# Two-layer cross-attention kernel, cross phase: the place of the attention products and of the last head's transposes in TensorE's order

## The reference, cut to what matters

```python
z = _mha(x1, context, Wq2, Wk2, Wv2, mask1, causal=False)
x2 = _layernorm(x1 + z, ln2_g, ln2_b)
z = jnp.maximum(x2 @ fc1_w.T + fc1_b, 0.0) * mask0
z = (z @ fc2_w.T + fc2_b) * mask0
return _layernorm(x2 + z, ln3_g, ln3_b)
# in _mha, for 16 heads of 32 channels:
energy = einsum('bhsk,bhtk->bhst', Q, K)
lengths = sum(energy[:, :, 0, :] != 0, axis=-1)
energy = where(cols >= lengths, -inf, energy)
out = einsum('bhst,bhtk->bhsk', softmax(energy / sqrt(32)), V)
```

## Time and profile before

| | |
|---|---|
| three runs | 2805.86, 2807.34, 2809.14 us, median 2807.34 |
| profiled execution | span 2805.9 us from first to last instruction, its own time |
| busy share of the span | PE 97%, PEld 84%, DVE 67%, ACT 58%, POOL 23% |
| TensorE's granted clock | 0.996 on average |
| cross phase | about 1963 to 2806 us, a turn of the loop some 51.03 us |

### The profile page before, as it was taken

One profiled execution on the slowest core, in us unless ns is written; L12 is line 12 of the kernel. 1 busy time (PEld: TensorE's weight loads), 2 busy tenths in 40 slices (PEclk: granted clock), 3 DMA queues, 4 the chain that ended last, 5 costly groups with the idle time before them and its releaser, 6 DMA issues.

```text
span 2805.9 us, 68735 instructions
## 1 busy us (share of the span) xinstructions
PE 2723.5 (97%) x24272; PEld 2360.1 (84%) x24272; DVE 1882.0 (67%) x5544; ACT 1634.7 (58%) x4949; POOL 637.8 (23%) x755
## 2 busy tenths in 40 slices
PE   6999999999999999999999999999999999999997
PEld 5888888887888888888888888888888888888886
DVE  6778778777544443445377777777677767767766
ACT  6878877888211111111277777777666666656664
POOL 1111111111000000000023333333233424324333
PEclk9999999999999999999999999999999999999999
DMA  3333332333302112012021111113111111101100
GB/s 119 108 99 99 106 112 86 106 107 99 124 30 60 45 45 60 30 60 88 33 83 51 47 45 45 45 45 105 36 45 37 37 45 45 39 36 45 45 30 24
DMA packets 145494, 178.45 MB, mean 64 GB/s; under 512 B 16272, under 2 KB 75664, under 8 KB 144912
## 3 DMA queue, kind: packets, MB, share of 16 engines
q1 hardware_dynamic: 145424, 177.53, 19.7%
HBM read 121.92 MB, written 55.57 MB: 63 GB/s over the span
## 4 chain that ended last, share of the span: by engine, by line
PE 40%; DVE 5%; issue 2%; ACT 2%; POOL 1%; POOLq 0%; DVEq 0%; ACTq 0%
PE cross_work L172 15%; PE causal_work L172 7%; PE cross_probsT L1961 2%; PE cross_attended L1980 2%; PE cross_scores L1940 2%; PE cross_scores L1961 2%; PE causal_attended L1980 1%; PE causal_scores L1961 1%; PE causal_scores L1940 1%; PE causal_probsT L1961 1%; PE cross_scores L1889 1%; DVE causal_scores L1323 1%; POOL causal_y L610 1%; PE causal_probsT L1922 1%; PE cross_probsT L1922 1%
## 5 line engine op out<-in xcount | busy, mean ns | idle before, releaser
L2804 ACT ACTIVATE mlp_h<-mlp_f,mlp_b1col 128x512 f32<-128x512 f32 x128 | 88.3, 690 | 526.7 <-PE mlp_f L3002 526.7
L3002 PE MATMUL mlp_f<-mlp_xT_hi,mlp_w 128*128 128x512 f32 x1024 | 335.1, 389 | 0.0
L3020 PE MATMUL mlp_acc<-mlp_w,mlp_hT_hi 128*128 128x512 f32 x1024 | 315.2, 389 | 0.0
L2905 DVE CAST mlp_hT_hi<-mlp_h 128x512 fp32r<-128x512 f32 x128 | 57.7, 451 | 375.3 <-ACT mlp_h L2804 375.2
L790 ACT ACTIVATE mask_prob<-mask_scores,mask_low 128x256 f32<-128x256 f32 x512 | 237.1, 475 | 21.5 <-DVE mask_low L1323 21.2
L790 ACT ACTIVATE cross_prob<-cross_scores,cross_low 128x256 f32<-128x256 f32 x512 | 237.5, 499 | 7.2 <-DVE cross_low L1317 7.0
L1323 DVE CUSTOM_DVE_ANT_0 mask_scores<-mask_scores,mask_mask 128x256 f32<-128x256 f32 x512 | 201.4, 457 | 46.4 <-PE mask_scores L1940 46.4
L172 PE MATMUL causal_work<-causal_xT_hi,causal_w 128*128 128x256 f32 x1008 | 227.6, 297 | 0.5
L3020 PEld LDWEIGHTS mlp_acc<-mlp_w,mlp_hT_hi 128*128 128x128 f32 x1024 | 192.3, 188 | 40.0
L3002 PEld LDWEIGHTS mlp_f<-mlp_xT_hi,mlp_w 128*128 128x128 f32 x1024 | 192.3, 188 | 39.8
L790 ACT ACTIVATE causal_prob<-causal_scores,causal_low 128x128 f32<-128x128 f32 (+1 forms) x512 | 211.3, 436 | 19.6 <-DVE causal_low L1323 19.6
(11 more groups left out here) (339 smaller groups left out, 8254.1 us busy)
## 6 DMA issues: line engine op xcount, KB each, us to landing
cross_x_in<-after_attention SPq DMA_DIRECT2D x17, 512.0 KB, 3.7
mask_x_in<-in_x SPq DMA_DIRECT2D x16, 512.0 KB, 4.7
mask_c_in<-in_ctx SPq DMA_DIRECT2D x16, 512.0 KB, 5.6
mask_res<-in_x SPq DMA_DIRECT2D x16, 512.0 KB, 3.6
after_attention<-mask_res SPq DMA_DIRECT2D x16, 512.0 KB, 2.8
mlp_x<-after_attention SPq DMA_DIRECT2D x8, 1024.0 KB, 5.6
mlp_stage<-in_L_xattn_fc_w SPq DMA_DIRECT2D x8, 1024.0 KB, 5.6
after_layer<-mlp_y SPq DMA_DIRECT2D x8, 1024.0 KB, 4.3
```

Source lines behind the costliest of these rows:

```text
L2804: act.activation(h32[:, m % 2, :], F1[m % 2][:], ACT.Gelu, bias=b1col[:, m:m + 1]).then_inc(s["gelu"], 1)
L3002: ins = pe.matmul(F1[m % 2][:], W[2 * (m // 4)][:, a, k, m % 4 * P:(m % 4 + 1) * P], xT[p][:, k, :], start=(k == 0 and n == 0), stop=(k == ...
L3020: ins = pe.matmul(ACC[t][:], hT[a][:, m % 2, t * P:(t + 1) * P], W[2 * (m // 4) + 1][:, p, m % 4, :], start=(m == 0 and n == 0), stop=(m = ...
```

## The change

The same instructions run on every engine, with another order on TensorE and two swaps on ACT; no instruction, wait value, tile or DMA is added or taken away. On TensorE, in the cross phase:

- T(-1) moves ahead of S(0), and A(-1) directly behind S(0); queries and keys follow as one run of 24 matmuls.
- The second half of `values(b, 0)` moves behind T(2); T(3) moves ahead of S(1); A(0) directly behind S(1), and queries behind A(0).
- T(10) moves up to directly behind A(1). The two halves of `feed1(b, 1)` stand behind it with OT(1) between them. T(11) stands behind the second half and ahead of S(3); A(2) directly behind S(3).
- T(14) moves ahead of the keys at the turn's end.
- A(1) is not moved to S(2).

On ACT, copy(2) moves ahead of `values(b, 0)` and copy(14) ahead of the next turn's `qk`. `feed1` raises `f1_ps` behind its second half alone, as it did.

```diff
--- before.py
+++ after.py
@@ -1045,8 +1045,8 @@
                 qk(b, 2)
                 copy(b, 0)
                 copy(b, 1)
+                copy(b, 2)
                 values(b, 0)
-                copy(b, 2)
 
                 copy(b, 3)
                 for u in (4, 5, 6):
@@ -1108,10 +1108,10 @@
                 copy(b, 13)
             if not prev:
                 matrix_hi(4, (2, 3))
+            if cur:
+                copy(b, 14)
             if nxt:
                 qk(b + 1, 1)
-            if cur:
-                copy(b, 14)
 
         def turn(b, prev, cur, nxt):
             if cross:
@@ -2019,7 +2019,7 @@
                 m = 2 * p + i
                 ins = product(pe, (W0 if p else W1)[:, i * S:(i + 1) * S],
                               lambda k, a: W[3][:, a, k, m * P:(m + 1) * P], lambda k, q: x2T[q][:, k, :])
-            if i:
+            if i == 1:
                 ins.then_inc(s["f1_ps"], 1)
 
         def feed2(b, t):
@@ -2386,17 +2386,12 @@
 
         def cross_turn(b, prev, cur, nxt):
 
-            if cur and prev:
+            if prev:
+                turn_probs(b, -1)
                 scores(b, 0)
-            if prev:
-                turn_probs(b, -1)
-            if cur and prev:
+                attend(b, -1)
                 pe.wait_ge(s["qk_lo"], KC * b + 2)
                 queries(b, 2)
-
-            if prev:
-                attend(b, -1)
-            if cur and prev:
                 keys(b, 2)
                 turn_probs(b, 0)
 
@@ -2409,20 +2404,18 @@
                 attended(b, -1)
 
             if cur:
-                values(b, 0, 1)
                 pe.wait_ge(s["len_ready"], KC * b + 2)
                 turn_probs(b, 2)
+                values(b, 0, 1)
+                turn_probs(b, 3)
 
             if cur:
                 scores(b, 1)
-                turn_probs(b, 3)
-                pe.wait_ge(s["qk_lo"], KC * b + 3)
-                queries(b, 3)
-
-            if cur:
                 if not prev:
                     pe.wait_ge(last["z_done"], KC * B + 1)
                 attend(b, 0)
+                pe.wait_ge(s["qk_lo"], KC * b + 3)
+                queries(b, 3)
                 keys(b, 3)
                 turn_probs(b, 4)
 
@@ -2482,35 +2475,29 @@
 
             if cur:
                 attend(b, 1)
-            if prev:
-                if cur:
-                    pe.wait_ge(s["v_ready"], 2 * b + 2)
-                else:
-                    pe.wait_ge(s["proj_read"], TT * (b - 1) + 1)
-                feed1(b, 1)
-            else:
-                pe.wait_ge(s["v_ready"], 2 * b + 2)
-                shift_through(1)
-            if cur:
-                attended(b, 1)
                 pe.wait_ge(s["len_ready"], KC * b + 4)
                 turn_probs(b, 10)
-
-            if cur:
+            pe.wait_ge(s["v_ready"], 2 * b + 2)
+            if prev:
+                feed1(b, 1, (0,))
+                attended(b, 1)
+                feed1(b, 1, (1,))
+            else:
+                shift_through(1)
+                attended(b, 1)
+
+            if cur:
+                turn_probs(b, 11)
                 if nxt:
                     pe.wait_ge(s["t_lo"], NP * (b + 2))
                 scores(b, 3)
-                turn_probs(b, 11)
+                attend(b, 2)
             if nxt:
                 if prev:
                     pe.wait_ge(s["f1_act"], 2 * (b - 1) + 1)
                 else:
                     pe.wait_ge(s["bias_done"], 1)
                 queries(b + 1, 0)
-
-            if cur:
-                attend(b, 2)
-            if nxt:
                 keys(b + 1, 0)
             if cur:
                 turn_probs(b, 12)
@@ -2532,12 +2519,13 @@
                 pe.wait_ge(s["proj_read"], TT * (b - 1) + 2)
                 feed2(b, 1)
             if nxt:
-                keys(b + 1, 1)
                 pe.wait_ge(s["len_ready"], KC * (b + 1) + 1)
             elif cur:
                 turned_free(b, 3)
             if cur:
                 turn_probs(b, 14)
+            if nxt:
+                keys(b + 1, 1)
 
         def turn(b, prev, cur, nxt):
             if cross and not cur:
```

More of the change, by code:

```diff
@@ L2387, in cross_turn @@
         def cross_turn(b, prev, cur, nxt):
-            if cur and prev:
-                scores(b, 0)
             if prev:
                 turn_probs(b, -1)
-            if cur and prev:
+                scores(b, 0)
+                attend(b, -1)
                 pe.wait_ge(s["qk_lo"], KC * b + 2)
                 queries(b, 2)
-            if prev:
-                attend(b, -1)
-            if cur and prev:
                 keys(b, 2)
```

## The result

The changed kernel takes 2829.72 us (median of 4 runs, 2827.46 to 2832.28), against 2806.6 (4 runs, 2805.74 to 2809.14): a ratio of 1.0083, 95% interval 1.007 to 1.0096. The profiled execution took 2827.46, with a span of 2825.7 us against 2805.9.

The account below looks back on a forecast made before the run. TensorE bounds, 97% busy. Turns 1 to 14 at +1.42 us each (+19.9), the last +1.3, turn 0 nothing: +21.2 on 2805.9 gives span 2827.1, and 1.4 more the median, 2828.5 us; range 2821 to 2840.

Parts of the forecast that it names:

- S to A: TensorE's seam between scores and the A behind them: gap taken as 0.20 us, S's own leaving gap; no row showed it.
- order alone: TensorE's new order without waits: three merged pairs and the stretch from A(1) to T(12) save 0.45 us a turn.
- hold at T(11): T(11) must wait for copy(10), which stands behind relu on ACT: TensorE stands for 1.67 us a turn.
- wait at S(2): S(2) waits 0.20 us a turn for cross_xT_lo, as the chain from S(1) takes 9.61 against TensorE's 9.41.
- a middle turn: Turns 1 to 14: 1.67 - 0.45 + 0.20 = +1.42 us each, +19.9 in all.
- last turn: It has the 1.67 hold, loses A(2)'s 0.69 wait, and T(12) waits some 0.8: about +1.3 us.
- turn 0: No relu there, and its end waits 1.94 us for POOL anyway: change of 0.
- third pair: S(3) with A(2), in the stretch A(1) to T(12): 10.22 us against 10.41, -0.19 a turn, 0.13 of it the pair's.
- The rule: At TensorE's mode changes: changing tiling mode drains the engine, so S to A drains too; alone it forecasts 2801 us.
- The covers: At T(3), A(0), A(-1): moved ACT copies still come in time, costing nothing; A(0) has 0.23 us to spare.
- The faster side: Rival at T(11): with copy(10) in time the merged pairs decide, -4.6 to -7.6 us, 2802.7 to 2799.7; chance 0.04.
- The fall of the clock: Rival behind the hold at T(11): clock falls each turn, up to 25 us more, 2854, or every second turn, 2841; chance 0.12.

Follow-up runs that it names:

- experiment 6: As experiment 1, plus DVE's two small operations (reciprocal, times zero) of chunk 2 moved behind the next low parts: 2802.96 us against 2807.39, ratio 0.9984.
- experiment 1: The changed kernel with one swap on ACT, copy(10) ahead of relu(b, 1): 2804.33 us against 2807.78 for the kernel before, ratio 0.9992.
- experiment 4: The kernel before with only TensorE's stretch from A(1) to the next keys changed: 2831.19 us against 2807.78, ratio 1.0087.
- experiment 3: The changed kernel with TensorE's stretch from A(1) to the keys put back, leaving two merged pairs: 2807.57 us against 2807.78, ratio 1.0001.
- experiment 9: The changed kernel with one more ACTIVATE of relu's size between relu(b, 1) and copy(10): 2851.16 us against 2806.76 for the kernel before, ratio 1.0161.
- experiment 5: The changed kernel with two more ACTIVATEs of relu's size between relu(b, 1) and copy(10): 2861.37 us against 2807.39 for the kernel before, ratio 1.0193.
- experiment 8: The kernel before, TensorE's order untouched, with copy(10) ahead of relu and DVE's two small operations behind the low parts: 2810.31 us against 2806.76, ratio 1.0012.

## Why the prediction was right

The forecast was 2828.5 us, the median is 2829.72. By the prediction's own steps, each with what was measured:

| step | forecast, us | measured, us |
|---|---|---|
| S to A, start to start | 1.15 (gap taken as 0.20, bounds -0.1 and +0.1) | 1.14 to 1.15 (gap 0.20) in all 47 cases |
| order alone, a turn | -0.45 | -0.44 (experiment 6 against before) |
| hold at T(11), a turn | +1.67 | last matmul's start to T(11) 1.79, less its 0.12 spacing: 1.67 |
| wait at S(2), a turn | +0.20 | T(6) to S(2) 0.745 against 0.529: +0.22 |
| a middle turn | +1.42 | +1.465 |
| last turn | +1.3 | +1.23 |
| turn 0 | 0 | -0.1, with the clock down twice in it before and once after |
| span | 2827.1 | 2825.7 |

**The hold.** Its chain was built from four prices of the profile before: release of relu 0.20, two ACTIVATEs 0.73, the copy 0.60, release of a waiting transpose 0.14. All four stand in the rows after. Experiment 1 takes away what makes T(11) wait and the turn gets 1.71 shorter; experiment 4 makes the hold alone and the turn gets 1.49 longer, which is the 1.67 less the 0.19 of the third pair. The waits view shows 22.6 us where the prediction named 25, since it counts 1.51 of the 1.67 as idle.

**The pairs.** The gap from S to A had no row in the trace before. The value 0.20 was taken, the gap that S leaves ahead of a transpose, and it came out so. The rule that the prediction took from the Trainium skill, "TensorEngine Tiling (Array Packing)", Tiling Modes, that a change of the tiling mode drains the engine, agrees: S works on row tiles and A on column tiles, and nothing was saved between them. Taken by itself the rule would have forecast a gain, since the kernel changes mode 47 times less; that gain is real, and the hold is nearly four times as large.

**S(2).** The prediction's chain from S(1) came to 9.61, measured 9.63. What the first two pairs gain ahead of S(2) is mostly given back there (experiment 3), and kept when DVE's stream lets the low part through earlier (experiment 6).

**The covers.** A(0), A(-1) and T(3) show no wait, as forecast. A(2) of the last turn lost its wait of 0.69, and T(12) behind it got one of 0.85, forecast 0.8.

**The sum.** The middle turn is 0.045 longer than forecast, 0.6 us in 14 turns: 0.03 is T(11)'s, whose transposes take 0.56 behind the hold, and 0.02 is S(2)'s. The span came 1.4 below the forecast because the stretch before the cross phase was 1.9 shorter in this execution. Against that, the median lies 4.0 above the span, where the prediction added 1.4. That 1.4 was taken from a median and a span of different executions; where a run has both, its time is 1.7 to 1.8 above its span, and the other 2.3 come from the other executions, which are longer at a lower mean clock (time 2827.46 at 0.997, 2829.72 at 0.995, 2832.28 at 0.994). So it is partly luck that 2828.5 met 2829.72 to 1.2 us: one error of -1.4 and one of +2.6 lie in it. What the prediction got right by its own working is the middle turn, +1.42 against +1.465.

**Turn 0 and the last turn.** That turn 0 came to nothing is not a clean confirmation. In the kernel before, the clock fell twice in it (0.57 over 1992 to 1996 and over 2009 to 2013), in the changed kernel once (0.57 over 1992 to 1996); experiment 9, whose turn 0 is that of the changed kernel, took 48.33 with the clock at 1.00 throughout, so the one fall in the changed kernel's cost 1.6. How long turn 0 of the kernel before takes with the clock up, no trace shows. Of the last turn's 1.23, 0.95 lie between S(0) and A(3); the other 0.28 come behind A(3), where no instruction was moved and the clock was down at other places.

**The rivals.** The faster side asked for a hold under 0.25 a turn; it needed copy(10) in time, and experiment 1 shows what that would have given: 14 turns of 0.24 less, 3.4 us, and a median 3.5 under that of the runs beside it, where the prediction had 4.6 to 7.6. Nothing is saved between S and A, and the 1.1 that it reckoned for the last turn was 0.4. The fall of the clock did not come with the change, at a hold of 1.67: the window behind T(11) has 1.00. The price of that rival leant on one case, the fall behind 1.94 us of standing in turn 0; behind 2.11 at the same place of the changed kernel there was none. The margin was thin all the same, as experiments 5 and 9 show: 0.36 us more of hold and it falls in most turns.

Not tried: A(1) behind S(2), the fourth pair (its output bank is also that of `post_turn`, so more than the order would have to move), and another bank for head 10's transposes, which would take T(11)'s wait away without moving relu.

## What to carry to other kernels

Before work is pulled together on the engine that bounds, take each wait that the moved piece has and look at what stands ahead of its release in the other engine's stream, and how long that something waits itself: here a copy of 0.60 us stood behind a relu which waited for a product that TensorE had just been given. Two orders written by hand belong together; moved alone, TensorE's lost 0.8% and ACT's and DVE's lost 0.1%, and moved together they won 0.2%. A gain ahead of a chain with no room (S(2) here) is worth only what that chain lets through, so the chain's other engines have to be moved as well.

## What the runs showed of the hardware

In these kernels the granted clock answered to a repeated hold that grew by a few tenths of a microsecond. Once a turn TensorE stood behind two dense products, and transposes and divided-array matmuls followed. With 1.67 us of standing the clock stayed at 2.4 GHz in all 14 middle turns; with 2.03 (experiment 9) it fell to 1.2 GHz behind the hold in 12 of 14, and in the last turn too; with 2.40 (experiment 5) in all but the first. Each of these counts is of one profiled execution. Each fall cost 1.5 us, four times the 0.36 us of hold that brought it: in experiment 9, 12 times 1.5 is 18 us of the 23 by which its 14 turns are longer than the changed kernel's.

The length of the hold doesn't decide alone. The two spared turns of experiment 9, 1 and 8, have the same idle as the others to 0.01 us; the fall began 0.4 us behind T(11)'s start in turn 2, some 0.25 later in each turn up to 1.6 in turn 7, then turn 8 was spared, and in turn 9 it began at 0.3 again. And at the end of turn 0, 2.11 us of idle were followed by a fall in experiment 8 (clock 0.77 over 2007 to 2013) and by none in the changed kernel (1.00). So where in time a hold falls seems to count beside its length; no run here separates the two.

Leaving S for A costs what leaving S for a transpose does: about 1.15 us from S's start in both cases (1.14 to 1.15 and 1.14 to 1.16). Two divided-array blocks of different kinds in a row thus save nothing at the seam between them, and only the entering and leaving on the far sides: 0.13 us a pair by the prices before. Experiment 3 agrees: two pairs less the 0.2 given back at S(2) would be 0.06 a turn, and its turn is 0.07 shorter than before.
